# A chunked state-space scan with its state update turned round, its exponents made in pairs, and its loop written out

## The chip, the cores and the metric

The kernel runs on one core of a Trainium2 chip. The time is device time from launch to end. The kernel before was timed three times: 3505.67, 3506.23 and 3528.6 us, median 3506.23 us.

## What is computed

Two layers on 2 x 2048 tokens of width 256: a state-space mixer, a mixture of experts, an attention without softmax, and a feed-forward with dequantized weights, each followed by a residual and a norm. The change touches the mixer, cut here to what matters (64 heads, 8 channels a head, 64 states):

```python
dt = softplus(dt_raw + dt_bias)
a = exp(-exp(A_log) * dt)
Bh = rope(rms(Braw) + B_bias, phi)          # phi = cumsum(dt) * rope_freqs, per head
Ch = rope(rms(Craw) + C_bias, phi)
u = xh * dt
def step(h, (a_t, u_t, b_t, c_t)):
    h = a_t * h + u_t outer b_t             # h: batch, head, 8 channels, 64 states
    y = einsum('bhpn,bhn->bhp', h, c_t)
```

## The kernel before

`project_and_decay` projects the tokens in 16 chunks of 128 tokens (both batches together) and writes B, C, phi, u, wu (u weighted by the decay to the end of the chunk), the running log decay in three bf16 pieces and their negatives, the decay since the chunk's start (et) and that of the whole chunk (dec) to scratch.

`state_space_scan` runs 64 steps t: 16 chunks c times 4 blocks k of 16 heads. A step has 4 quarters q of four heads (8 groups g of two heads, two groups a quarter). Chunks 0 and 15 are written out, chunks 1 to 14 are a hardware loop of four steps a pass. Each engine has its own list, written by hand and tied by semaphores:

- ScalarE: `in_turns`, `whole_turns` (three activations a quarter), `magnitude`, `sines` make sine and cosine of the angles three and two steps ahead; the sine needs one table and the exponential another, so two table loads a step. `decays` turns a bank of exponents into decays D (L837); `turned` copies a bank of turned B into BT (L843).
- SyncE: `expand` spreads sine and cosine over partitions with 16 DMAs a step; `load_g` fetches the exponent pieces, `load_phi`, `load_u`, `load_wu`, `load_last` the rest. One queue in order.
- VectorE: `products` (four operations a group, L914 and L920), then `decayed`: M = scores times D, a bank each (L928), `outputs`, `new_state` (four small operations: state times dec, plus the new part).
- GpSimd: adds the products to C and B turned by the angle (CR L627, BR L633), spreads u into uexp, subtracts whole turns (L618).
- TensorE, by line: `exponents` (one 512-column bf16 mask matmul at L662 over all rows and two 256-column ones of 15 rows at L665, for one bank; eight banks a step), `turned` (four 128x128 fp32 transposes, L676), `scores` (eight fp32 matmuls in two halves of the rows, L688), `outputs` (`of_chunk` L703 and `of_state` L696, 32 columns of the array each), `new_state` (four fp32 matmuls with the turned B as the stationary side and 16 moving columns, L733). An fp32 matmul that isn't a transpose is two passes, two records in the trace.

Exponents and turned B share two PSUM banks, `x_ps[0]` and `x_ps[1]`, in turn: an item may be written when the item two before it has been read by ScalarE (`at_least(e, S["x_ok"], t, per, i - 1)`). The score banks `sc_ps` are single.

## Time and profile before

| | |
|---|---|
| median of three runs | 3506.23 us |
| the profiled execution, time / span | 3547.34 / 3545.6 us |
| busy share of the span: TensorE, VectorE, ScalarE, GpSimd | 80%, 57%, 43%, 40% |
| mean granted clock of TensorE | 0.776 |
| `project_and_decay` | to about 222 us |
| the scan | 225 to about 2206 us |
| the rest | 2206 to 3545 us |

The profile is one execution; the granted clock is 1.0 at 2.4 GHz and 0.5 at 1.2 GHz. Records on TensorE overlap, since matmuls are pipelined: a group of matmuls is best read from the start of one row to the start of the next. A few matmul records are missing (half of those of L662), which shows as idle time with "issue" behind it.

### The profile page before, as it was taken

To read this page: it belongs to the slowest core of one execution; us is meant where nothing else is said; L and a number is where in the kernel's file an instruction comes from. 1 tells how busy PE (TensorE), PEld (TensorE's weight loads), DVE (VectorE), ACT (ScalarE), POOL (GpSimd) and SP (SyncE) were. 2 spreads that over 40 slices of the span, in tenths; PEclk is the share of its full clock that TensorE was granted. 3 is DMA by queue.
4 is the path that set the end of the run, shared out by engine and by line. 5 is a ranking of instruction groups with operands and counts; after the bars stand their busy time and mean duration, and the time that the engine had idled before them with its cause. 6 is when DMAs were issued, how large, how long until landed. Compare 5 with 4: busy or idle time off the path is not lost. (4 is left out here: it accounts for less than half of the span.)

```text
span 3545.6 us, 70494 instructions
## 1 busy us (share of the span) xinstructions
PE 2838.9 (80%) x20132; PEld 2130.3 (60%) x20386; DVE 2018.2 (57%) x5459; ACT 1542.2 (43%) x3010; POOL 1435.4 (40%) x2256
## 2 busy tenths in 40 slices
PE   7848888888888888888888888888683885775888
PEld 4526666666666666666666666677562443553887
DVE  4546666656666665666666665333462222774777
ACT  4455555555565555656665553111450111221222
POOL 2236554545554454555555453000240111441544
PEclk9876676766676676767776667899786998887999
DMA  5654444444444444444444443322343222333111
GB/s 152 181 159 118 114 113 115 116 103 110 108 113 98 116 116 105 116 112 114 111 118 112 99 99 82 96 91 92 117 139 125 68 70 85 105 112 110 36 44 39
DMA packets 320535, 374.69 MB, mean 106 GB/s; under 512 B 71314, under 2 KB 260980, under 8 KB 319796
## 3 DMA queue, kind: packets, MB, share of 16 engines
q1 hardware_dynamic: 310404, 344.02, 37.1%
q0 software_dynamic: 9872, 27.28, 2.3%
q8 instruction: 155, 2.54, 0.3%
q14 instruction: 104, 0.85, 0.1%
HBM read 150.33 MB, written 86.58 MB: 67 GB/s over the span
## 5 line engine op out<-in xcount | busy, mean ns | idle before, releaser
L627 POOL TENSOR_TENSOR p_CR<-p_pc 128x256 f32<-128x256 f32 x512 | 372.8, 728 | 713.7 <-DVE p_pc L914 653.9
L928 DVE TENSOR_TENSOR p_M<-p_ps_sc,p_D 128x512 f32<-128x512 f32 x512 | 329.6, 686 | 562.6 <-PE p_ps_sc L688 561.6
L688 PE MATMUL p_ps_sc<-p_CR,p_BR 64*128 64x128 f32 x4096 | 445.6, 381 | 4.7 <-POOL p_BR L633 4.3
L843 ACT ACTIVATE p_BT<-p_ps_x 128x512 f32<-128x512 f32 x256 | 151.5, 592 | 619.6 <-PE p_ps_x L676 619.6
L688 PEld LDWEIGHTS p_ps_sc<-p_CR,p_BR 64*128 64x128 f32 x4096 | 382.2, 276 | 60.6 <-issue 40.5
L703 PE MATMUL p_ps_y<-p_M,p_uexp 128*32 128x128 f32 x4096 | 374.0, 342 | 31.4 <-issue 31.4
L837 ACT ACTIVATE p_D<-p_ps_x 128x512 f32<-128x512 f32 x512 | 303.7, 594 | 195.6 <-PE p_ps_x L665 127.1
L633 POOL TENSOR_TENSOR p_BR<-p_pb 128x256 f32<-128x256 f32 x512 | 371.8, 726 | 37.4 <-DVE p_pb L920 22.7
L733 PEld LDWEIGHTS p_ps_ns<-p_wu,p_BT 128*128 128x128 f32 x2048 | 335.7, 249 | 73.5 <-issue 52.5
L733 PE MATMUL p_ps_ns<-p_wu,p_BT 128*128 128x16 f32 x2048 | 361.5, 312 | 0.0
L676 PE MATMUL p_ps_x<-p_ident,p_BR 128*128 128x128 f32 x1024 | 224.4, 358 | 138.6 <-ACT p_D L837 138.6
L665 PE MATMUL p_ps_x<-p_GR,p_GL 15*128 15x256 bf16 x1024 | 244.2, 327 | 109.4 <-issue 63.3
L703 PEld LDWEIGHTS p_ps_y<-p_M,p_uexp 128*32 128x32 f32 x4096 | 265.4, 136 | 73.4 <-issue 37.0
L914 DVE SCALAR_TENSOR_TENSOR p_pc<-p_ps_c,p_beta,p_cs 128x256 f32<-128x256 f32 x512 | 243.8, 476 | 54.6 <-DMA p_sn<-p_tr_s 25.5
L618 POOL TENSOR_TENSOR p_tr_s<-p_xt,p_mg 128x256 f32<-128x256 f32 x256 | 186.9, 730 | 203.5 <-ACT p_mg L818 203.5
L696 PE MATMUL p_ps_y<-p_CR,p_ST 128*32 128x128 f32 x2048 | 264.9, 347 | 0.0
L676 PEld LDWEIGHTS p_ps_x<-p_ident,p_BR 128*128 128x128 f32 x1024 | 144.2, 178 | 195.9 <-ACT p_D L837 139.4
L920 DVE SCALAR_TENSOR_TENSOR p_pb<-p_ps_b,p_beta,p_cs 128x256 f32<-128x256 f32 x512 | 243.3, 475 | 0.0
L914 DVE SCALAR_TENSOR_TENSOR p_pc<-p_ps_c,p_beta,p_sn 128x256 f32<-128x256 f32 x512 | 243.3, 475 | 0.0
L920 DVE SCALAR_TENSOR_TENSOR p_pb<-p_ps_b,p_beta,p_sn 128x256 f32<-128x256 f32 x512 | 243.3, 475 | 0.0
L665 PEld LDWEIGHTS p_ps_x<-p_GR,p_GL 15*128 15x128 bf16 x1024 | 59.1, 97 | 179.6 <-issue 179.6
L1677 PE MATMUL p_ps_up<-p_w,p_xT 128*128 x288 | 130.3, 576 | 43.7 <-issue 43.0
(279 smaller groups left out, 5324.8 us busy)
## 6 DMA issues: line engine op xcount, KB each, us to landing
p_cs<-p_tr_c SPq DMA_DIRECT2D x512, 128.0 KB, 2.4
p_sn<-p_tr_s SPq DMA_DIRECT2D x512, 128.0 KB, 2.4
p_phib<-scratch_phi SPq DMA_DIRECT2D x256, 128.0 KB, 2.9
p_x<-scratch_rt SPq DMA_DIRECT2D x72, 128.0 KB, 2.0
scratch_ro<-p_o POOLq DMA_DIRECT2D x72, 128.0 KB, 2.0
p_xT<-in_xT SPq DMA_DIRECT2D x64, 128.0 KB, 3.0
scratch_u<-p_u SPq DMA_DIRECT2D x16, 512.0 KB, 3.8
scratch_wu<-p_wu SPq DMA_DIRECT2D x16, 512.0 KB, 5.0
```

Source lines behind the costliest of these rows:

```text
L627: e.tensor_tensor(CR[:, p, g, :], pc[:, g % 2, 0, :], pc[:, g % 2, 1, :], ALU.add).then_inc(S["rotC"], 1)
L633: e.tensor_tensor(BR[:, g, :], pb[:, g % 2, 0, :], pb[:, g % 2, 1, :], ALU.add).then_inc(S["rotB"], 1)
L665: m = e.matmul(bank[:, :].rearrange("p (g b l) -> p g b l", g=2, b=BATCH)[:, :, b, :], GL[:, p, cols], GR[:, p, half:4:2, cols], start=Fal ...
L676: m = e.transpose(x_ps[i % 2][:, (g * 2 + b) * P:(g * 2 + b + 1) * P], BR[:, 2 * q + g, b * L:(b + 1) * L], ident[:, :])
L688: m = e.matmul(sc_ps[half][:, (g * 2 + b) * L:(g * 2 + b + 1) * L], BR[half * 64:half * 64 + 64, 2 * q + g, b * L:(b + 1) * L], CR[half * ...
L696: m = e.matmul(yx_ps[32 * q:32 * q + 32, b * L:(b + 1) * L], ST[:, k, q, b, g, :], CR[:, k % 2, 2 * q + g, b * L:(b + 1) * L], start=(g == ...
L703: m = e.matmul(yi_ps[32 * q:32 * q + 32, b * L:(b + 1) * L], uexp[:, p, b, 4 * q + h, :], M[:, m_slot(p, 2 * q + h % 2), (h // 2 * 2 + b) ...
L733: m = e.matmul(ns_ps[:, ((q * 2 + b) * 2 + g) * 16:((q * 2 + b) * 2 + g) * 16 + 16], BT[:, q, g * 2 + b, :], wu[:, p, b, (2 * q + g) * 16: ...
L837: e.activation(D[:, n, :], x_ps[i % 2][:, :], ACT.Exp).then_inc(S["x_ok"], 1)
L914: e.scalar_tensor_tensor(out=pc[:, g % 2, n - 2, :], in0=c_ps[:, (n - 2) * CT:(n - 1) * CT], scalar=beta[:, k, n, g:g + 1], in1=tr[:, p, g ...
L920: e.scalar_tensor_tensor(out=pb[:, g % 2, n, :], in0=b_ps[:, n * CT:(n + 1) * CT], scalar=beta[:, k, n, g:g + 1], in1=tr[:, p, g % 2, g // ...
L928: e.tensor_tensor(M[:, m_slot(p, n), :], sc_ps[n % 2][:, :], D[:, n, :], ALU.mult).then_inc(S["m_ok"], 1)
```

## The change

- `project_and_decay` no longer makes the decay of the whole chunk: one 128-column fp32 matmul, half of the exponent product, one exponential, two copies and one DMA a chunk go. `sufA_ok` is then signalled once a chunk.
- The state is held twice. SR is the state turned: partitions are (head, channel), the free side the 128 state rows; VectorE updates it from PSUM in two operations a step, with the last column of et as its decay. `state(t - 2)` transposes it on TensorE through one of the two shared banks, and ScalarE copies the needed blocks to ST, which `of_state` reads as before.
- `new_state` is one group a step: wu is the stationary side in four column tiles of 32, the turned B moves with 256 columns. Eight matmuls instead of sixteen.
- `exponents` makes two banks at once: the mask as four matmuls of 256 columns in two halves of the rows, the exponents as four of 256 columns with 16 rows each at rows 0 and 32. It waits until both banks have been read. Its operands come with eight DMAs a step instead of six; that of dec is gone.
- No loop: all 64 steps are written out on all engines, with constants for waits and addresses. The last four steps make no new state.
- The order within a step is new on TensorE, ScalarE and GpSimd.

```diff
-                at_least(e, S["sufA_ok"], t, 2, 0)
+                at_least(e, S["sufA_ok"], t, 1, 0)
                 for b in range(BATCH):
                     e.matmul(ph_ps[0:NH, b * L:(b + 1) * L], dtp[:, b, :], triu[:, :], start=True, stop=True)
                     e.matmul(ph_ps[0:NH, CT + b * L:CT + (b + 1) * L], dt[:, b, :], triu[:, :], start=True, stop=True)
-                e.matmul(cum_ps[:, 0:2 * NH], tril[:, :], dt[:, :, :].rearrange("p b h -> p (b h)"), start=True, stop=True)
-                e.matmul(cum_ps[:, 2 * NH:4 * NH], ones[:, :], dt[:, :, :].rearrange("p b h -> p (b h)"),
-                         start=True, stop=True).then_inc(S["cum_mm"], 1)
+                e.matmul(cum_ps[:, 0:2 * NH], tril[:, :], dt[:, :, :].rearrange("p b h -> p (b h)"), start=True, stop=True
+                         ).then_inc(S["cum_mm"], 1)
...
-                at_least(e, S["dec_ok"], t, 1, 0)
-                for n in range(2):
-                    e.tensor_tensor(expo[:, n, :, :], cum_ps[:, n * 2 * NH:(n + 1) * 2 * NH].rearrange("p (b h) -> p b h", b=BATCH),
-                                    repeat(nA_bc[:, :], BATCH), ALU.mult).then_inc(S["sufA_ok"], 1)
+                e.tensor_tensor(expo[:, :, :], cum_ps[:, 0:2 * NH].rearrange("p (b h) -> p b h", b=BATCH),
+                                repeat(nA_bc[:, :], BATCH), ALU.mult).then_inc(S["sufA_ok"], 1)
...
-                for h in range(2):
-                    e.tensor_copy(decx[h * 64:(h + 1) * 64, p, :, :, :],
-                                  dec[h * 64:(h + 1) * 64, :, :].rearrange("p b (q e h) -> p q b e h", e=2, h=2)[:, :, :, :, h]
-                                  ).then_inc(S["decx_ok"], 1)
...
-        GR = sb("GR", [15, 2, 4, NQ * CT], BF16)
-        GL = sb("GL", [15, 2, NQ * CT], BF16)
+        GR = sb("GR", [48, 2, 2, NQ * CT], BF16)
+        GL = sb("GL", [48, 2, NQ * CT], BF16)
...
-        ST = sb("ST", [P, NB, NQ, BATCH, 2, 32])
+        SR = sb("SR", [P, NB, BATCH, 2, P])
+        ST = sb("ST", [P, NB, 2, BATCH, P])
...
+        order = [("D", 0, n) for n in range(4)]
+        for t in range(T):
+            order += [("B", t - 1, 2)] * (1 <= t <= LAST) + [("D", t, 4), ("D", t, 5)]
+            order += [("B", t - 1, 3)] * (1 <= t <= LAST) + [("D", t, 6), ("D", t, 7)]
+            order += [("S", t - 2, 0)] * (2 <= t < LAST + 2) + [("B", t, 0)] * (t < LAST)
+            order += [("D", t + 1, 0), ("D", t + 1, 1)] * (t + 1 < T) + [("B", t, 1)] * (t < LAST)
+            order += [("D", t + 1, 2), ("D", t + 1, 3)] * (t + 1 < T)
+        place = {item: i for i, item in enumerate(order)}
...
+                for half in range(2):
+                    r = 32 * half
+                    e.dma_start(GR[r:r + 3, p, :, :], W["pieces"][c].rearrange("a (h k q) t -> a h k (q t)", h=4, k=NB)[:, half:4:2, k, :]
+                                ).then_inc(g_in[p], 16)
+                    for a in range(3):
+                        e.dma_start(GL[r + 3 + 4 * a:r + 7 + 4 * a, p, :],
+                                    W["negs"][c, a].rearrange("(h k q) t -> h k (q t)", h=4, k=NB)[:, k, :]).then_inc(g_in[p], 16)
...
-                    stage_u(t, p, g // 2, g % 2)
-                    if 1 <= g <= NQ and ahead:
-                        turns(t + 2, p, g - 1)
+                    if g % 2:
+                        if g < NG - 1 and t + 2 < T:
+                            turns(t + 2, p, g // 2 + 1)
+                        if g == NG - 1 and t + 3 < T:
+                            turns(t + 3, 1 - p, 0)
+                        for b in range(BATCH):
+                            stage_u(t, p, g // 2, b)
...
+            def exponents(t, p, q):
+                n = 2 * q
+                i = place["D", t, n]
                 if n == 0:
+                    at_least(e, g_in[p], t - p, 8 * 8, 16 * 8)
+                at_least(e, S["x_ok"], i, 1, 0)
+                bank = [x_ps[(i + half) % 2] for half in range(2)]
+                for turn in range(2):
+                    for half in range(2):
+                        r = slice(64 * half, 64 * half + 64)
+                        e.matmul(bank[half][:, :].rearrange("p (n l) -> p n l", l=L)[:, :, 64 * turn:64 * turn + 64], eye[r, turn, :],
+                                 repeat(low[r, :], 4), start=(turn == 0), stop=False)
+                for b in range(BATCH):
+                    at = slice(q * CT + b * L, q * CT + b * L + L)
+                    for half in range(2):
+                        r = 32 * half
+                        m = e.matmul(bank[half][:, :].rearrange("p (g b l) -> p g b l", g=2, b=BATCH)[:, :, b, :], GL[r:r + 16, p, at],
+                                     GR[r:r + 16, p, :, at], start=False, stop=(b == 1))
+                        if b:
+                            m.then_inc(S["x_mm"], 1)
...
+
+            def state(t):
+
+                i = place["S", t, 0]
+                at_least(e, S["st_ok"], t, 2, 2)
+                at_least(e, S["x_ok"], i, 1, -1)
+                for g in range(2):
+                    for b in range(BATCH):
+                        m = e.transpose(x_ps[i % 2][:, (g * 2 + b) * P:(g * 2 + b + 1) * P], SR[:, t % NB, b, g, :], ident[:, :])
...
+            def new_state(t, p):
+                at_least(e, S["x_ok"], place["B", t, NQ - 1], 1, 1)
+                at_least(e, wu_got[p], t - p, 8, 16)
+                at_least(e, S["st_ok"], t, 2, 0)
+                for b in range(BATCH):
+                    for q in range(NQ):
+                        m = e.matmul(ns_ps[32 * q:32 * q + 32, b * CT:(b + 1) * CT], wu[:, p, b, 32 * q:32 * q + 32],
+                                     BT[:, q, b:4:2, :], start=True, stop=True)
+                        if b:
+                            m.then_inc(S["ns_mm"], 1)
...
-                later = not (isinstance(t, int) and t == 0)
-                more = not (isinstance(t, int) and t == T - 1)
-                if later:
-                    outputs(l, lk, 0, 1)
+                kept, more = t <= LAST, t + 1 < T
+                scores(t, p, 0)
+                if t and kept:
                     turned(l, 2)
-                scores(t, p, 0)
-                if later:
-                    exponents(t, p, 4)
-                    exponents(t, p, 5)
-                    new_state(l, lp, 1)
+                exponents(t, p, 2)
+                if t:
                     outputs(l, lk, 1, 0)
+                scores(t, p, 1)
+                if t and kept:
                     turned(l, 3)
-                scores(t, p, 1)
-                exponents(t, p, 6)
-                exponents(t, p, 7)
-                if later:
-                    new_state(l, lp, 2)
+                exponents(t, p, 3)
+                if t:
                     outputs(l, lk, 1, 1)
-                    new_state(l, lp, 3)
                 scores(t, p, 2)
-                turned(t, 0)
+                if t and kept:
+                    new_state(l, lp)
+                if 2 <= t < LAST + 2:
+                    state(t - 2)
+                if t < LAST:
+                    turned(t, 0)
                 if more:
                     exponents(t + 1, 1 - p, 0)
-                    exponents(t + 1, 1 - p, 1)
                 outputs(t, k, 0, 0)
                 scores(t, p, 3)
-                turned(t, 1)
+                if t < LAST:
+                    turned(t, 1)
+                outputs(t, k, 0, 1)
                 if more:
-                    exponents(t + 1, 1 - p, 2)
-                    exponents(t + 1, 1 - p, 3)
-                new_state(t, p, 0)
-
+                    exponents(t + 1, 1 - p, 1)
...
+            for t in range(T):
+                step(t, t % NB, t // NB)
...
+                if t and t <= LAST:
+                    turned(t - 1, 2)
+                for q in range(2):
+                    if q and t and t <= LAST:
+                        turned(t - 1, 3)
+                    decays(t, 4 + 2 * q)
...
+            def state(t):
+
+                i = place["S", t, 0]
+                at_least(e, S["x_mm"], i, 1, 1)
+                at_least(e, S["yx_mm"], t, U, U)
+                for h in range(2):
+                    r = slice(h * 64, h * 64 + 64)
+                    def own(ap):
+                        return bass.AP(tensor=ap.tensor, offset=ap.offset, ap=[list(ap.ap[0]), [2 * P + 16, 2], [32, BATCH * NQ], [1, HD]])
+                    e.activation(own(ST[r, t % NB, 0, 0, h * HD:h * HD + HD]), own(x_ps[i % 2][r, h * HD:h * HD + HD]), ACT.Copy
+                                 ).then_inc(S["x_ok" if h else "kept"], 1)
...
-                for h in range(2):
-                    r = slice(h * 64, h * 64 + 64)
-                    e.tensor_tensor(state_blocks(k, r, h), state_blocks(k, r, h),
-                                    spread(dec[r, p, :].rearrange("p (n e) -> p n e", e=2), HD), ALU.mult).then_inc(S["st_dec"], 1)
+                at_least(e, et_in[p], t - p, 8, 16)
                 at_least(e, S["ns_mm"], t, NQ, NQ)
-                at_least(e, S["st_dec"], t, 2, 2)
-                for h in range(2):
-                    r = slice(h * 64, h * 64 + 64)
-                    e.tensor_tensor(state_blocks(k, r, h), state_blocks(k, r, h),
-                                    ns_ps[r, 0:NQ * BATCH * 32].rearrange("p (n e d) -> p n e d", e=2, d=16)[:, :, :, h * HD:(h + 1) * HD],
-                                    ALU.add).then_inc(S["st_ok"], 1)
+                if t >= NB:
+                    e.wait_ge(S["x_mm"], place["S", t - NB, 0] + 1)
+                for b in range(BATCH):
+                    s = SR[:, k, b, :, :].rearrange("p g n -> p (g n)")
+                    e.scalar_tensor_tensor(out=s, in0=s, scalar=et[:, p, b * L + L - 1:b * L + L], in1=ns_ps[:, b * CT:(b + 1) * CT],
+                                           op0=ALU.mult, op1=ALU.add).then_inc(S["st_ok"], 1)
...
```

TensorE, one middle step before, from the third scores group (names: ps_sc scores, ps_x the shared banks, ps_ns the new state, ps_y outputs):

```order
L688 MATMUL p_ps_sc<-p_CR,p_BR 128x128 x8
L676 MATMUL p_ps_x<-p_ident,p_BR 128x128 x4
L662 MATMUL p_ps_x<-p_mask,p_identb 128x512
L665 MATMUL p_ps_x<-p_GR,p_GL 128x2x128 x2
L662 MATMUL p_ps_x<-p_mask,p_identb 128x512
L665 MATMUL p_ps_x<-p_GR,p_GL 128x2x128 x2
L703 MATMUL p_ps_y<-p_M,p_uexp 32x128 x4
L696 MATMUL p_ps_y<-p_CR,p_ST 32x128 x2
L703 MATMUL p_ps_y<-p_M,p_uexp 32x128 x4
L696 MATMUL p_ps_y<-p_CR,p_ST 32x128 x2
L688 MATMUL p_ps_sc<-p_CR,p_BR 128x128 x8
```

The same place now:

```order
L692 MATMUL p_ps_sc<-p_CR,p_BR 128x128 x8
L738 MATMUL p_ps_ns<-p_BT,p_wu 32x256 x8
L681 MATMUL p_ps_x<-p_ident,p_SR 128x128 x4
L670 MATMUL p_ps_x<-p_ident,p_BR 128x128 x4
L652 MATMUL p_ps_x<-p_low,p_eye 128x4x64 x4
L658 MATMUL p_ps_x<-p_GR,p_GL 128x2x128 x4
L707 MATMUL p_ps_y<-p_M,p_uexp 32x128 x4
L700 MATMUL p_ps_y<-p_CR,p_ST 32x128 x2
L707 MATMUL p_ps_y<-p_M,p_uexp 32x128 x4
L700 MATMUL p_ps_y<-p_CR,p_ST 32x128 x2
L692 MATMUL p_ps_sc<-p_CR,p_BR 128x128 x8
```

The four groups of new state that stood apart are one behind the third scores, the state's transposes follow, and the pair of banks is filled by one group of eight.

ScalarE around the sines before (D decays, BT turned B, xt and mg the turns of the angles, tr_s and tr_c sine and cosine):

```order
L843 ACTIVATE p_BT<-p_ps_x 128x512
L822 ACTIVATE p_tr_c<-p_tr_s 128x512
L828 ACT_TABLE_LOAD
L828 ACTIVATE p_tr_c<-p_tr_c,p_quart 128x512 x2
L831 ACTIVATE p_tr_s<-p_tr_s 128x512 x2
L837 ACT_TABLE_LOAD
L837 ACTIVATE p_D<-p_ps_x 128x512
L811 ACTIVATE p_xt<-p_phib,p_fsc 128x256
L837 ACTIVATE p_D<-p_ps_x 128x512
```

And now:

```order
L829 ACTIVATE p_D<-p_ps_x 128x512
L803 ACTIVATE p_xt<-p_phib,p_fsc 128x256
L829 ACTIVATE p_D<-p_ps_x 128x512
L808 ACTIVATE p_mg<-p_phib,p_fsc 128x256
L810 ACTIVATE p_mg<-p_mg 128x256
L814 ACTIVATE p_tr_c<-p_tr_s 128x512
L820 ACT_TABLE_LOAD
L820 ACTIVATE p_tr_c<-p_tr_c,p_quart 128x512 x2
L823 ACTIVATE p_tr_s<-p_tr_s 128x512 x2
L835 ACTIVATE p_BT<-p_ps_x 128x512
L829 ACT_TABLE_LOAD
L829 ACTIVATE p_D<-p_ps_x 128x512
```

The copy of turned B that stood ahead of the sines stands behind them, ahead of the second table load.

## Rows read from the trace of the kernel before

**Rows 1.** Busy time by stretch: length, PE, PEld, DVE, ACT, POOL, clock, DMA, GB/s.

```profile
428.20:2106.90 1678.70, 1442.38 (x12542) 1068.65 (x12761) 1078.97 (x2530) 978.55 (x1816) 866.65 (x1540) 0.70 0.46 111
2206.00:3545.00 1339.00, 989.10 (x4865) 776.22 (x4865) 636.90 (x2174) 304.15 (x705) 359.53 (x402) 0.87 0.28 89
```

**Rows 2.** Instruction groups, 428 to 2107 us: busy us, mean ns | idle before, releaser.

```profile
L928 DVE TENSOR_TENSOR p_M<-p_ps_sc,p_D 128x512 f32<-128x512 f32 x440 | 283.3, 686 | 495.6 <-PE p_ps_sc L688 494.8
L676 PE MATMUL p_ps_x<-p_ident,p_BR 128*128 128x128 f32 x880 | 194.3, 360 | 121.0 <-ACT p_D L837 121.0
```

**Rows 3.** TensorE in order of time at clock 1.0: start, length, instruction, count.

```profile
1007.05 0.39 PE L665 MATMUL p_ps_x<-p_GR,p_GL 15*128 15x256 bf16 x2 [0.26 <-issue]
1007.69 0.39 PE L665 MATMUL p_ps_x<-p_GR,p_GL 15*128 15x256 bf16 x2
1008.00 1.06 PE L733 MATMUL p_ps_ns<-p_wu,p_BT 128*128 128x16 f32 x8
1009.00 0.30 PE L703 MATMUL p_ps_y<-p_M,p_uexp 128*32 128x128 f32 x2
...
1010.00 1.06 PE L733 MATMUL p_ps_ns<-p_wu,p_BT 128*128 128x16 f32 x8
...
1016.40 1.16 PE L688 MATMUL p_ps_sc<-p_CR,p_BR 64*128 64x128 f32 x16
1017.49 0.66 PE L676 MATMUL p_ps_x<-p_ident,p_BR 128*128 128x128 f32 x4
```

**Rows 4.** The same at clock 0.5.

```profile
1032.90 0.60 PE L665 MATMUL p_ps_x<-p_GR,p_GL 15*128 15x256 bf16 x2 [0.48 <-issue]
1033.97 0.60 PE L665 MATMUL p_ps_x<-p_GR,p_GL 15*128 15x256 bf16 x2
1034.50 1.89 PE L733 MATMUL p_ps_ns<-p_wu,p_BT 128*128 128x16 f32 x8
1036.32 0.43 PE L703 MATMUL p_ps_y<-p_M,p_uexp 128*32 128x128 f32 x2
...
1038.17 1.89 PE L733 MATMUL p_ps_ns<-p_wu,p_BT 128*128 128x16 f32 x8
1039.99 2.08 PE L688 MATMUL p_ps_sc<-p_CR,p_BR 64*128 64x128 f32 x16
1042.01 1.11 PE L676 MATMUL p_ps_x<-p_ident,p_BR 128*128 128x128 f32 x4
```

**Rows 5.** Busy time by stretch, between changes of the granted clock.

```profile
1024.30:1031.10 6.80, 4.56 (x57) 3.35 (x58) 4.42 (x10) 6.74 (x11) 2.36 (x5) 1.00 0.36 80
1031.10:1048.20 17.10, 16.27 (x120) 11.97 (x122) 10.84 (x26) 6.54 (x14) 7.83 (x14) 0.50 0.56 135
```

**Rows 6.** ScalarE in order of time, around the sines.

```profile
1024.48 1.28 ACT L828 ACT_TABLE_LOAD   x1
...
1029.46 0.60 ACT L837 ACTIVATE p_D<-p_ps_x 128x512 f32<-128x512 f32 x1
...
1031.69 0.58 ACT L843 ACTIVATE p_BT<-p_ps_x 128x512 f32<-128x512 f32 x1
```

**Rows 7.** VectorE in order of time: outputs of steps 0 and 4, written-out steps.

```profile
304.71 0.42 DVE L954 TENSOR_TENSOR p_y<-p_ps_y,p_yx 128x256 f32<-128x256 f32 x1
...
428.20 0.42 DVE L954 TENSOR_TENSOR p_y<-p_ps_y,p_yx 128x256 f32<-128x256 f32 x1
```

**Rows 8.** VectorE in order of time, one quarter of a step.

```profile
1014.88 0.48 DVE L914 SCALAR_TENSOR_TENSOR p_pc<-p_ps_c,p_beta,p_cs 128x256 f32<-128x256 f32 x1
...
1018.03 1.28 DVE L928 TENSOR_TENSOR p_M<-p_ps_sc,p_D 128x512 f32<-128x512 f32 x2
1019.22 0.47 DVE L914 SCALAR_TENSOR_TENSOR p_pc<-p_ps_c,p_beta,p_cs 128x256 f32<-128x256 f32 x1
```

**Rows 9.** SyncE's queue in order of time.

```profile
1002.13 5.25 SPq L521 DMA_DIRECT2D p_cs<-p_tr_c  x8
```

**Rows 10.** Instruction groups of the first phase, 20 to 220 us.

```profile
L399 DVE COPY p_decx<-p_dec 64x64 f32<-64x64 f32 x32 | 21.1, 661 | 0.5
```

More of the change, by code:

```diff
@@ L584, in _ @@
                 step(k, k, 0)
-            with e.Fori(1, NC - 1) as c:
+            for c in range(1, NC - 1):
                 for k in range(NB):
@@ L771, in step @@
-                new_state(t, p, 0)
-            for n in range(EARLY):
-                exponents(0, 0, n)
-            for k in range(NB):
-                step(k, k, 0)
-            with e.Fori(1, NC - 1) as c:
-                for k in range(NB):
-                    step(c * NB + k, k, c)
-            for k in range(NB):
-                step(T - NB + k, k, NC - 1)
-            t, k, p = T - 1, NB - 1, 1
-            outputs(t, k, 0, 1)
-            turned(t, 2)
-            turned(t, 3)
-            new_state(t, p, 1)
@@ L879, in _ @@
                 sines(s, s)
-            for n in range(EARLY):
+            for n in range(4):
                 decays(0, n)
@@ L884, in _ @@
                 step(k, k, 0)
-            with e.Fori(1, NC - 1) as c:
+            for c in range(1, NC - 1):
                 for k in range(NB):
@@ L976, in _ @@
                 step(k, k, 0)
-            with e.Fori(1, NC - 1) as c:
+            for c in range(1, NC - 1):
                 for k in range(NB):
```

271 lines of the change are left out of this document (118 added, 153 removed).

## The prediction

> **What bounds the kernel now.** I read the table of stretches first. The 55 steps between 428 and 2107 us take 1678.7 us, 30.5 each; per step TensorE is busy 26.2 us, VectorE 19.6, ScalarE 17.8, GpSimd 15.8 [rows 1]. So TensorE carries most of the scan, and at a mean granted clock of 0.70: two fifths of the time at 2.4 GHz, three fifths at 1.2. The list of groups says the same from the other side: VectorE's largest wait is for scores (495 us), TensorE's own largest visible one is 121 us for ScalarE to free a shared bank [rows 2]. Then I read TensorE in order of time, once at either clock, start of group to start of group.
>
> At 2.4 GHz [rows 3]: one bank of exponents 0.64, a group of new state 1.00, of outputs 1.00, of scores 1.09, of turned B 0.59 (0.66 less the 0.07 that overlaps the next). At 1.2 GHz [rows 4]: 1.07, 1.82, 1.85, 2.02, 1.04. A step has eight banks and four of each other group: 5.1 + 4.0 + 4.0 + 4.4 + 2.4 = 19.8 us fast; 8.6 + 7.3 + 7.4 + 8.1 + 4.2 = 35.5 us slow. Half of each is 27.6, near the 26.2 us busy. The other 4.3 us are waits.
>
> **TensorE's work after.** Scores, turned B and outputs stay: 10.7 fast, 19.6 slow.
> *New state.* Four groups go (4.0, 7.3). One comes: eight matmuls of two passes, 256 columns each, in four column tiles. No row has just this form. Nearest are the outputs, also four column tiles of 32: there the longest tile has eight passes of 128 columns, here four of 256, the same 1024 columns. I take 1.0 fast, 1.9 slow. If the tiles ran one after the other it would be four times that, 4.0 and 7.4: no gain.
> *Exponents.* A bank streams 512 + 2 x 256 = 1024 columns in 0.64 us; at 2.4 GHz the columns alone are 0.43. A pair of banks now streams eight times 256 columns, two at a time in different rows: again 1024 if the pairs run side by side. Scores are made of such halves: sixteen passes take 1.09 us where four whole-array passes take 0.59 [rows 3], so halves do overlap. Bounds for a pair: 0.64 (1.07) and 1.28 (2.14). I take 0.75 (1.3), near the lower end because of the scores, more than it for the extra weight loads. Four pairs: 3.0 and 5.2 instead of 5.1 and 8.6.
> TensorEngine Tiling of the Trainium skill, Key Properties, says that changing the tiling mode drains the engine. The 0.21 us above the columns in a bank would be two such changes; by that rule new modes beside old ones could cost some 0.1 us each, but the changes inside the exponents halve from sixteen to eight, so by it the pair is no dearer than I take.
> *State.* Four transposes, as turned B: 0.6, 1.0.
> Sum: 10.7 + 1.0 + 3.0 + 0.6 = 15.3 fast; 19.6 + 1.9 + 5.2 + 1.0 = 27.7 slow. TensorE loses 4.5 to 7.8 us a step.
>
> **What becomes late next.** (a) A pair waits for both banks. Three of the four pairs stand right behind a group of turned B, so TensorE waits until ScalarE has copied that: 0.58 us of copy [rows 6] and two hand-overs, about 0.8. That is 2.4 us a step, where before the second bank alone waited.
> (b) The sines. Behind the first pair ScalarE does D, xt, D, mg, mg (2.2 us, as from 1029.5 to 1031.7), an absolute value (0.6), table and sines (4.98 less the second load of 1.28: 3.7), the copy (0.6) [rows 6]: 7.1 us until the second pair may start. TensorE has outputs, scores, turned B, outputs to do: 3.7 us fast, 6.7 slow. So it idles 3 to 4 us fast, under 1 slow.
> (c) VectorE. A quarter of products takes 3.15 us, two banks of M 1.19 [rows 8]; four quarters, outputs (1.0) and the state make 19.4. Two state operations of 128x256, one source in PSUM, replace four of half the partitions: bounds nothing and twice 0.48, so at most 0.4 moves either way.
>
> Chain at 2.4 GHz from the end of the third scores: new state, state, turned B 2.2, copy 0.8, pair 0.75: 3.8. ScalarE 7.1: 11. Pair and scores: 13. Now VectorE: M 1.2, products 3.15, M 1.2, products 3.15, outputs 1.0: **22.7**, when the next third M comes. At 1.2 GHz TensorE has no rest: 27.7 + 2.4 + 0.8 = **31**.
>
> **The clock.** From 1024.3 to 1031.1 TensorE was busy for 4.56 of 6.8 us at 1.0, then the clock fell, and from 1031.1 to 1048.2 it was busy for 16.27 of 17.1 us at 0.5 [rows 5]. The stages behind the scan are at 0.87, busy for 989 of 1339 us [rows 1]. So these rows don't tell what other work in the scan will be granted; (b) opens an idle stretch each step at 1.0, as the one before the fall. I take the middle between the scan's 0.70 and the later 0.87: 0.78, 56% of the time fast. Step: 1 / (0.56/22.7 + 0.44/31) = 25.7 us. With 0.70: 27.1; with 0.9: 24.0.
>
> **The rest.** *No loop:* the four written-out steps from 304.71 to 428.20 took 30.9 us each, the looped ones 30.5 [rows 7, 1]. So writing out is worth nothing by itself. *SyncE:* two DMAs more, one less; eight of the sixteen DMAs that spread sine and cosine take 5.25 us to issue [rows 9], the 16 of them 10.5, and the other 16 to 18 of a step no more each: at most some 21 in one queue, below 25.7, without much to spare. Its wait for new state moves back by one scores group. *GpSimd:* same work, 15.8 us. *First phase:* the copies are 21.1 us in all [rows 10] and stand on VectorE between u and the next chunk's v, but TensorE's sum of squares ends nearly as late; between 0 and 22 us, I take 6. *Last four steps:* no turned B, new state, state (4 us less each for three) and the shorter step: 25.
> Sum: 60 steps x (30.5 - 25.7) = 288, + 25 + 6 = 319 us. The profiled execution took 3547.34 us; 3547 - 319 = 3228. It stands 41 us above the median of the runs, so against that: **3190 us**.
>
> **Rivals.**
> 1. *Forecast*, steps of 24 to 28.9 us, 3090 to 3390: chance 0.62.
> 2. *The clock stays up* through the idle stretch; then VectorE's chain of 22.7 rules: 60 x 7.8 + 50 = 518 less, 2990. For it: 0.87 behind the scan [rows 1]. Against: the idle stretch each step. 0.15.
> 3. *The clock falls.* Every step has an idle stretch after which the clock drops, and 31 us at 1.2 GHz is nearly reached: steps of 29 to 31, 3390 to 3510, priced 3450. For it: [rows 5]. Against: at 1.2 GHz the idle stretch shrinks to under 1 us, and before, the clock rose again in each step. 0.15. TensorE: Matmul & The Clock Gate (HAM oscillation) says that idle gaps between bursts put the clock back; by that rule it would be this rival, 3450, and this trace agrees at 1031.1.
> 4. *Slower: tiles do not run side by side.* New state 4.0 (7.4) and pairs 1.28 (2.14) make 20.4 fast and 36.7 slow, against 19.8 and 35.5 now: 0.9 us more work a step, and (a) adds 2.4, with all else kept a step of 33: 60 x 2.8 - 30 = +140, 3640. It decides once the gained overlap is worth less than the 2.4 us of new waits. Against it: outputs and scores overlap in just these tilings [rows 3]. 0.08.
>
> About 1% (35 us) is what a measurement here can tell from no change. Faster by more (under 3471): rivals 1, 2 and half of 3: 0.85. Same: 0.08. Slower: 0.07. The range reaches from 3000 to 3430: all of the forecast's own 3090 to 3390, the upper half of rival 2 and the lower half of rival 3.
>
> **What would show it.** Steps of 25 to 26 us between outputs. New state as one group of 1.0 (1.9) us; four to twice that would be rival 4. A pair of banks in 0.75 (1.3) us. TensorE idle before each pair: three times 0.8 for ScalarE's copy, once several us behind the sines. A clock of 0.78 in the scan: above 0.9 is rival 2, below 0.6 rival 3. VectorE's wait for scores down from 9 us a step to 6. The forecast is wrong if a DMA ends VectorE's waits, which would be SyncE's queue, or if VectorE's busy time grows by more than 0.4 us a step.

## The result, and the profile after

| | before | after |
|---|---|---|
| median, four runs each | 3517.41 us | 3166.49 us |
| lowest to highest | 3505.67 to 3550.91 | 3158.88 to 3191.54 |
| ratio, 95% interval | | 0.8998, 0.8924 to 0.9072 |
| profiled execution, time / span | 3547.34 / 3545.6 us | 3191.54 / 3189.9 us |
| first to last output of the scan | 304.7 to 2205.1: 1900.4 us | 321.8 to 1845.5: 1523.7 us |

A tenth of the time is gone: 3190 was forecast. Two further executions of the changed kernel took 3186.52 and 3149.3 us, so its six reach from 3149 to 3192 us, and the profiled one, 3191.54, is the slowest of them, 25 us above the median, so its steps are some 0.4 us longer than those of the median run (25 over 64 steps, an estimate). A run more than 1.5% above the fastest of its kernel counts as slow here, which holds for three of the four of a_halfwait below and for two of the four of a_single_both and of a_filler_busy. By the profiles the span lost 355.7 us: 376.7 between the first and the last output of the scan; ahead of it 17.1 came on top, behind it 3.9. Inside the scan the last four steps gave 30.6 (98.1 us before, 67.5 after, from output to output), the other 59 gave 346.1, 5.87 each (30.55 before, 24.68 after).

The stretches of after (length, PE, PEld, DVE, ACT, POOL, clock, DMA, GB/s), which answer to [rows 1]:

```profile
11.00:222.00 211.00, 180.54 (x603) 118.51 (x604) 92.37 (x270) 89.11 (x164) 52.59 (x43) 0.80 0.53 154
430.00:1778.00 1348.00, 1017.26 (x12408) 696.47 (x12409) 1043.26 (x2398) 992.84 (x1908) 875.92 (x1524) 0.79 0.56 137
1850.00:3189.00 1339.00, 991.49 (x4865) 778.77 (x4865) 635.52 (x2171) 302.98 (x705) 359.83 (x400) 0.87 0.28 89
```

In the scan TensorE is busy for 75% of the time, VectorE now for 77% and ScalarE for 74%: no engine stands out any more. The clock is 0.79, from 0.70. The outputs come in a pattern of four, 23.7, 23.8, 25.8 and 25.7 us, mean 24.75, which repeats through the scan:

```profile
887.11 0.42 DVE L971 TENSOR_TENSOR p_y<-p_ps_y,p_yx 128x256 f32<-128x256 f32 x1
912.81 0.42 DVE L971 TENSOR_TENSOR p_y<-p_ps_y,p_yx 128x256 f32<-128x256 f32 x1
936.52 0.42 DVE L971 TENSOR_TENSOR p_y<-p_ps_y,p_yx 128x256 f32<-128x256 f32 x1
960.32 0.42 DVE L971 TENSOR_TENSOR p_y<-p_ps_y,p_yx 128x256 f32<-128x256 f32 x1
986.11 0.43 DVE L971 TENSOR_TENSOR p_y<-p_ps_y,p_yx 128x256 f32<-128x256 f32 x1
```

TensorE in order of time, against [rows 3] and [rows 4]. A pair of banks at 2.4 GHz, with the new state and the state behind it; then a pair at 1.2 GHz:

```profile
989.69 0.39 PE L652 MATMUL p_ps_x<-p_low,p_eye 64*128 64x256 bf16 x4 [0.93 <-ACT p_BT L835]
990.02 0.39 PE L658 MATMUL p_ps_x<-p_GR,p_GL 16*128 16x256 bf16 x4
990.34 0.30 PE L707 MATMUL p_ps_y<-p_M,p_uexp 128*32 128x128 f32 x2
...
997.51 0.61 PE L652 MATMUL p_ps_x<-p_low,p_eye 64*128 64x256 bf16 x4 [3.42 <-ACT p_BT L835]
998.05 0.61 PE L658 MATMUL p_ps_x<-p_GR,p_GL 16*128 16x256 bf16 x4
998.59 0.58 PE L692 MATMUL p_ps_sc<-p_CR,p_BR 64*128 64x128 f32 x2
...
1010.98 1.07 PE L738 MATMUL p_ps_ns<-p_BT,p_wu 128*32 128x256 f32 x16
1011.98 0.66 PE L681 MATMUL p_ps_x<-p_ident,p_SR 128*128 128x128 f32 x4
```

Start to start: a pair takes 0.65 us (989.69 to 990.34) and 1.08 (997.51 to 998.59), all new state of a step 1.00 where four groups of that length stood. The brackets are the waits for ScalarE's copy of turned B. The long one, 3.42 us, is there because the copy stands behind the sines. ScalarE in order of time:

```profile
992.67 0.61 ACT L814 ACTIVATE p_tr_c<-p_tr_s 128x512 f32<-128x512 f32 x1
993.30 1.28 ACT L820 ACT_TABLE_LOAD   x1
994.60 1.33 ACT L820 ACTIVATE p_tr_c<-p_tr_c,p_quart 128x512 f32<-128x512 f32 x2
995.84 1.13 ACT L823 ACTIVATE p_tr_s<-p_tr_s 128x512 f32<-128x512 f32 x2
996.88 0.57 ACT L835 ACTIVATE p_BT<-p_ps_x 128x512 f32<-128x512 f32 x1
```

The groups, 430 to 1778 us (busy us, mean ns | idle before, releaser), against [rows 2]:

```profile
L950 DVE TENSOR_TENSOR p_M<-p_ps_sc,p_D 128x512 f32<-128x512 f32 x436 | 280.1, 684 | 283.1 <-PE p_ps_sc L692 283.0
L652 PE MATMUL p_ps_x<-p_low,p_eye 64*128 64x256 bf16 x872 | 106.3, 330 | 326.6 <-ACT p_BT L835 326.6
```

Eight M a step, so the 436 are 54.5 steps: VectorE waits 5.2 us a step for scores instead of 9, TensorE 6.0 for the copies. All of that is near the forecast, which says nothing yet on why the time fell. The experiments take that up. Where a kernel is called "the changed kernel with ...", all else is as in it.

### The profile page after: what moved, and what is told of

Read it like the earlier page. It is cut to its first block and busy times, and to the rows that moved or that the text cites. A ratio compares the mean times of both kernels' runs of the same rounds, so it can differ in the third digit from the quotient of the medians.

```text
span 3189.9 us, 63590 instructions
## 1 busy us (share of the span) xinstructions
PE 2361.8 (74%) x19953; PEld 1713.3 (54%) x19954; DVE 1962.2 (62%) x5279; ACT 1555.5 (49%) x3098; POOL 1455.4 (46%) x2255
## 5 line engine op out<-in xcount | busy, mean ns | idle before, releaser
L652 PE MATMUL p_ps_x<-p_low,p_eye 64*128 64x256 bf16 x1024 | 124.8, 330 | 408.2 <-ACT p_BT L835 359.6
L692 PE MATMUL p_ps_sc<-p_CR,p_BR 64*128 64x128 f32 x4096 | 377.7, 336 | 13.4 <-POOL p_BR L615 7.8
L615 POOL TENSOR_TENSOR p_BR<-p_pb 128x256 f32<-128x256 f32 x512 | 373.5, 730 | 25.8
L692 PEld LDWEIGHTS p_ps_sc<-p_CR,p_BR 64*128 64x128 f32 x4096 | 322.4, 236 | 86.3 <-issue 49.3
L707 PE MATMUL p_ps_y<-p_M,p_uexp 128*32 128x128 f32 x4096 | 341.7, 321 | 5.1 <-POOL p_uexp L592 3.9
L652 PEld LDWEIGHTS p_ps_x<-p_low,p_eye 64*128 64x128 bf16 x1024 | 34.1, 100 | 479.9 <-ACT p_BT L835 360.0
L707 PEld LDWEIGHTS p_ps_y<-p_M,p_uexp 128*32 128x32 f32 x4096 | 244.7, 128 | 82.4 <-issue 65.3
L670 PE MATMUL p_ps_x<-p_ident,p_BR 128*128 128x128 f32 x960 | 187.8, 328 | 4.6 <-ACT p_D L829 3.1
L1660 POOL DMA_DIRECT2D scratch_ro<-p_o x72 | 39.2, 544 | 276.3 <-DVE p_o L1764 272.5
L1758 DVE TENSOR_TENSOR p_h<-p_sa,p_ps_up 128x224 f32<-128x224 f32 x72 | 27.9, 388 | 190.7 <-ACT p_sa L1739 190.7
L2298 ACT ACTIVATE p_sg<-p_ps_g,p_gs 128x256 f32<-128x256 f32 x128 | 53.8, 471 | 185.7 <-PE p_ps_g L2236 185.7
```

Source lines behind the costliest of these rows:

```text
L615: e.tensor_tensor(BR[:, g, :], pb[:, g % 2, 0, :], pb[:, g % 2, 1, :], ALU.add).then_inc(S["rotB"], 1)
L652: e.matmul(bank[half][:, :].rearrange("p (n l) -> p n l", l=L)[:, :, 64 * turn:64 * turn + 64], eye[r, turn, :], repeat(low[r, :], 4), sta ...
L670: m = e.transpose(x_ps[i % 2][:, (g * 2 + b) * P:(g * 2 + b + 1) * P], BR[:, 2 * q + g, b * L:(b + 1) * L], ident[:, :])
L692: m = e.matmul(sc_ps[half][:, (g * 2 + b) * L:(g * 2 + b + 1) * L], BR[half * 64:half * 64 + 64, 2 * q + g, b * L:(b + 1) * L], CR[half * ...
L707: m = e.matmul(yi_ps[32 * q:32 * q + 32, b * L:(b + 1) * L], uexp[:, p, b, 4 * q + h, :], M[:, m_slot(p, 2 * q + h % 2), (h // 2 * 2 + b) ...
```

## The experiments

Twelve kernels, with the changed kernel in the first row. Each ratio is to the kernel before, run beside it on the same chip. The kernels of the table did not all run on one chip, so two of them are best compared by their ratios, and the clock is that of one profiled execution each.

| kernel | median, us (lowest to highest) | ratio, 95% interval | clock, 430 to 1630 us |
|---|---|---|---|
| the changed kernel | 3166.5 (3158.9 to 3191.5) | 0.8998, 0.8924 to 0.9072 | 0.79 |
| b_unrolled | 3570.8 (3565.2 to 3572.6) | 1.0125, 1.0080 to 1.0171 | 0.67 |
| a_oldboth | 3198.3 (3197.9 to 3212.2) | 0.9109, 0.9067 to 0.9151 | 0.80 |
| a_oldstate | 3288.6 (3281.8 to 3299.1) | 0.9323, 0.9268 to 0.9379 | 0.77 |
| a_single | 3131.3 (3128.2 to 3141.3) | 0.8889, 0.8836 to 0.8942 | 0.84 |
| a_single_both | 3335.5 (3278.6 to 3365.3) | 0.9345, 0.9230 to 0.9460 | 0.76 |
| a_halfwait | 3186.2 (3136.3 to 3189.7) | none given | 0.79 |
| a_oldphase0 | 3158.6 (3149.5 to 3161.9) | 0.8959, 0.8918 to 0.8999 | 0.82 |
| a_copy_first | 3135.0 (3132.1 to 3147.3) | 0.8883, 0.8815 to 0.8951 | 0.86 |
| a_filler | 3129.9 (3129.2 to 3130.4) | 0.8860, 0.8795 to 0.8924 | 0.86 |
| a_filler_busy | 3250.9 (3207.9 to 3275.0) | 0.9268, 0.9213 to 0.9324 | 0.88 |
| a_copy_filler | 3128.6 (3121.6 to 3138.2) | 0.8907, 0.8865 to 0.8948 | 0.94 |
| a_copy_single | 3212.3 (3209.6 to 3220.6) | 0.9133, 0.9097 to 0.9170 | 0.82 |

### The loop alone: b_unrolled

```diff
-            with e.Fori(1, NC - 1) as c:
+            for c in range(1, NC - 1):
```

> The kernel before with its five hardware loops of the scan written out, and nothing else. My theory (the gain is less TensorE work and better overlap, the loop costs nothing): steps of 30 to 31 us, the time within 1% of before, 3480 to 3555. Rival (the loop costs each engine a stop at every fourth step): steps of 29 or less, 60 us or more gone, under 3455.

Slower by 1.25%, which neither theory had: the rival expected a gain, mine a time within 1%. The steps themselves are nearly as long as before: almost all 30.7 us, one like the other, where the looped ones vary between 26 and 34 with a mean of 30.5. In the profiles 13.0 us of the 24.2 come ahead of the first output (317.7 for 304.7) and 10.8 in the scan. The first phase, whose code is the same, differs from 55 us on; the kernel before, then this one:

```profile
55.00:100.00 45.00, 36.79 (x159) 23.74 (x158) 27.76 (x81) 24.08 (x47) 12.94 (x11) 0.99 0.72 205
```

```profile
55.00:100.00 45.00, 40.37 (x128) 26.12 (x127) 21.98 (x64) 18.53 (x36) 11.23 (x10) 0.73 0.55 156
```

At 0.73 instead of 0.99 TensorE gets through 128 matmuls instead of 159. All written-out kernels here have their first output later than 304.7, at 309.1 to 329.1. But the clock of this stretch is no mark of the written-out loop: with the same first phase it is 0.97 in a_oldboth, 0.85 in a_oldstate and 0.82 in a_oldphase0, each in one execution. What makes the clock fall earlier in some of them was not found.

### The order without the lighter work: a_oldboth, a_oldstate

a_oldstate puts the old state back (and with it the old first phase); a_oldboth fills banks singly as well, so that TensorE again has the work of the kernel before.

```diff
-                for b in range(BATCH):
-                    for q in range(NQ):
-                        m = e.matmul(ns_ps[32 * q:32 * q + 32, b * CT:(b + 1) * CT], wu[:, p, b, 32 * q:32 * q + 32],
-                                     BT[:, q, b:4:2, :], start=True, stop=True)
+                for q in range(NQ):
+                    for g in range(2):
+                        for b in range(BATCH):
+                            m = e.matmul(ns_ps[:, ((q * 2 + b) * 2 + g) * 16:((q * 2 + b) * 2 + g) * 16 + 16], BT[:, q, g * 2 + b, :],
+                                         wu[:, p, b, (2 * q + g) * 16:(2 * q + g) * 16 + 16], start=True, stop=True)
...
-                if 2 <= t < LAST + 2:
-                    state(t - 2)
```

> The changed kernel with the old handling of the state: sixteen narrow fp32 matmuls of new state, here in one place, VectorE's four small operations with the decay of the whole chunk, no transposes of the state, and the first phase of before. Pairs, order and written-out steps stay. My theory (TensorE's work decides): four groups of 1.0 (1.82) instead of one of 1.01 and a transpose group of 0.6 (1.0): 2.4 us fast and 4.4 us slow more a step, a third of it hidden in the idle stretch behind the sines: steps of 26.5 to 28.5, the time 3270 to 3400. Rival (pairs and order made the whole gain): 3150 to 3210.

> The new order and the written-out steps alone: single banks as in a_single, the old handling of the state and the old first phase as in a_oldstate. TensorE then has the work of the kernel before, 19.8 us a step at 2.4 GHz and 35.5 at 1.2. Theory A (the forecast's sum: less work in TensorE is the gain): nothing is left of it, 3480 to 3570, steps of 29.5 to 31. Theory B (the order is most of the gain: single banks cost nothing in it, the old state 120 to 140 us): 3230 to 3300, steps of 25 to 26.5, at a clock of 0.80 or more in the scan.

a_oldstate came where the theory had it, which looked like support for it. a_oldboth overturns it: with the whole old work on TensorE the time is 3198 us, below even theory B's range. The same stretch, 430 to 1630 us, and groups of it, of the kernel before:

```profile
430.00:1630.00 1200.00, 1030.09 (x8962) 762.83 (x9116) 771.49 (x1810) 697.50 (x1296) 617.32 (x1097) 0.70 0.46 111
...
L928 DVE TENSOR_TENSOR p_M<-p_ps_sc,p_D 128x512 f32<-128x512 f32 x316 | 203.4, 686 | 356.0 <-PE p_ps_sc L688 355.5
L676 PE MATMUL p_ps_x<-p_ident,p_BR 128*128 128x128 f32 x632 | 139.5, 359 | 85.2 <-ACT p_D L837 85.2
```

and of a_oldboth:

```profile
430.00:1630.00 1200.00, 1157.71 (x11499) 821.71 (x11492) 934.04 (x2206) 844.75 (x1582) 770.76 (x1343) 0.80 0.56 136
...
L938 DVE TENSOR_TENSOR p_M<-p_ps_sc,p_D 128x512 f32<-128x512 f32 x384 | 246.8, 685 | 152.6 <-PE p_ps_sc L698 151.4
L743 PE MATMUL p_ps_ns<-p_wu,p_BT 128*128 128x16 f32 x1536 | 210.0, 285 | 0.0
L686 PE MATMUL p_ps_x<-p_ident,p_BR 128*128 128x128 f32 x768 | 158.8, 342 | 4.1 <-ACT p_D L831 3.3 <-POOL p_BR L633 0.4
```

316 and 384 M in the same time: 39.5 steps and 48, or 30.4 and 25.0 us each. TensorE is busy for 86% and 96% of the time; its wait of 85 us for ScalarE to read an exponent bank is 3.3; VectorE waits 3.2 us a step for scores instead of 9.0. Two things stand side by side here, and the rows allow an estimate of their shares. With 19.8 us of work at 2.4 GHz and 35.5 at 1.2, and four tenths of the time fast, as clock 0.70 says, a step is 1 / (0.4/19.8 + 0.6/35.5) = 27.0 us of work; with six tenths, clock 0.80, it is 24.1. So some 2.9 us of the 5.4 are the clock and the rest, 2.5, is idle time of TensorE that went.

This kernel keeps more of the change than the order: the steps written out (which alone cost), new state's groups in one place, the mask in halves. It does without the two parts that make TensorE's work less. Which of the moves within the order brings how much was not tried one by one.

### The pairs: a_single, a_single_both, a_halfwait

```diff
-                at_least(e, S["x_ok"], i, 1, 0)
-                bank = [x_ps[(i + half) % 2] for half in range(2)]
-                for turn in range(2):
-                    for half in range(2):
+                for half in range(2):
+                    at_least(e, S["x_ok"], i + half, 1, -1)
+                    bank = x_ps[(i + half) % 2]
+                    for turn in range(2):
```

and so on for the exponents: a_single fills one bank, then the other. a_single_both does the same behind one wait for both banks, `at_least(e, S["x_ok"], i, 1, 0)`. a_halfwait moves that wait into the masks' loop over banks and leaves the exponent matmuls in pairs. Its masks are then filled bank by bank and no longer run side by side: its TensorE is busy for 992 of the 1200 us, that of the changed kernel for 906.

> The changed kernel, its order and halves of rows kept, but the two banks of a pair filled one after the other, each when it is free. My theory (paired row tiles run side by side): the pair's 0.65 us becomes 1.28 and 1.08 becomes 2.1, so four pairs cost TensorE 2.5 to 4 us more a step, part of it given back because the first bank no longer waits for the second (three waits of 0.8): steps of 26 to 28 against 24.75, the time 3240 to 3370. Rival (the gain is all order and new state, the pairs are worth nothing, since the wait for both banks eats it): 3140 to 3190, as the changed kernel.

> The kernel with single banks (a_single, 3131 us, steps of 23.3, TensorE busy 20.4 us a step at clock 0.84), but each pair again waits for both banks before its first bank is filled. Theory A (the changed kernel's pairs lose by the wait for both banks, three times 0.8 us a step): the gain of a_single is gone: steps of 24.5 or more, 3190 or more, since the longer fill of 1.28 us comes on top. Theory B (they lose by the clock: less work in TensorE lets it fall, and more work keeps it up): the clock stays at 0.83 or above, steps of 23.3 to 24.2, 3130 to 3180.

> The changed kernel with pairs, but the mask of the first bank goes out when that bank is free, ahead of the wait for the second; the exponent matmuls stay paired. Theory A (the wait for both banks): some 0.3 us of four waits a step leave the path, steps of 23.7 to 24.4 against 24.75, 3130 to 3170, at an unchanged clock. Theory B (the clock): no change beyond what the clock does, 3150 to 3195 at 0.79.

Both theories on a_single were wrong: it is faster than the changed kernel. The difference is small, about 1% by the ratios, whose intervals just overlap, but the slowest of its four runs (3141.3 us) lies 8 us below the fastest of that kernel's six (3149.3). The price of two banks is as expected, 0.63 us each; TensorE of a_single in order of time:

```profile
983.52 0.38 PE L652 MATMUL p_ps_x<-p_low,p_eye 64*128 64x256 bf16 x2 [0.31 <-ACT p_ST L887]
983.83 0.39 PE L657 MATMUL p_ps_x<-p_GR,p_GL 16*128 16x256 bf16 x2
984.15 0.39 PE L652 MATMUL p_ps_x<-p_low,p_eye 64*128 64x256 bf16 x2
984.47 0.39 PE L657 MATMUL p_ps_x<-p_GR,p_GL 16*128 16x256 bf16 x2
```

So TensorE has 2.5 us more work a step, and the steps are 23.7 instead of 24.8 (by the estimate above some 0.4 us of that is the changed kernel's profile, which isn't its median run). With the old state the pairs cost even more: a_oldstate is 90 us behind a_oldboth. a_single_both shows what they cost by: the same fills, but behind the wait for both banks, and its fastest run is 137 us above a_single's slowest. The wait is what hurts. VectorE's wait for scores goes from 197.5 to 342.8 us of the 1200, 3.9 to 8.0 us a step, so the late pair is passed on to it. Theory B, steps of 24.2 at most at a clock that stays up, is refuted by the time; the 0.76 of the table is from its slowest run, 3365 us. Filling side by side makes good a part of what that wait costs, not all of it. a_halfwait decides nothing: three of its runs are at 3184 to 3190 us, one at 3136, on either side of the changed kernel's median, and what its earlier first mask could gain stands against masks that are no longer side by side.

### The idle stretch and the clock: a_copy_first, a_filler, a_filler_busy, a_copy_filler

a_copy_first, ScalarE's list:

```diff
+                if t < LAST:
+                    turned(t, 1)
                 if t + 2 < T:
                     magnitude(t + 2, p, 1)
                     sines(t + 2, p)
-                if t < LAST:
-                    turned(t, 1)
```

a_filler, TensorE's list, with GB a tile of ones; in a_filler_busy the same stands behind `scores(t, p, 2)`, in a_copy_filler twelve of them behind `scores(t, p, 0)`:

```diff
                 outputs(t, k, 0, 1)
+                if 1 <= t < LAST:
+                    at_least(e, S["st_ok"], t, 2, 0)
+                    for n in range(8):
+                        e.matmul(ns_ps[:, :], eye[:, 0, :], GB[:, :], start=True, stop=True)
                 if more:
                     exponents(t + 1, 1 - p, 1)
```

> The changed kernel with ScalarE's copy of the second turned B back ahead of the magnitude and the sines, as in the kernel before. Theory (the wait of the second pair, 3.4 us a step, is for this copy, which stands behind 3.7 us of sines): TensorE can start the pair 3 us sooner, but ScalarE must wait for scores and turned B ahead of the sines, 1.9 us at 2.4 GHz and 3.9 at 1.2, and is then late for the next exponentials: between 1 us a step gained and 2 lost, 3100 to 3290, most likely 3200 with the clock above 0.82. Rival (the sines' place costs nothing, VectorE sets the step): 3155 to 3185.

> The changed kernel plus eight bf16 matmuls of 512 columns a step that nothing reads, some 1.7 us at 2.4 GHz and 3.4 at 1.2, put on TensorE where it waits 3.4 us for ScalarE behind the sines. Theory B (idle stretches cost the clock): the granted clock in the scan goes from 0.79 to 0.84 or more and the steps from 24.75 to 23 to 24: 3060 to 3140. Rival (TensorE has no time to give): the filler lengthens the steps that run at 1.2 GHz, 3190 to 3260.

Useless work in the idle stretch makes the kernel 37 us faster than the changed one, and its four runs lie within 1.2 us. The steps are 23.9 and the clock 0.86, as theory B had it; the clock still falls once in each step, though TensorE's longest wait is now 2.0 us. a_copy_first gains 32 us without extra work, in the time's own range but better than its likeliest value. Both are about 1%: all their runs lie below all six of the changed kernel, while the intervals of the ratios touch or overlap. In a_copy_first every step but the first few is 23.9, and the clock falls once in each. Two of its stretches between changes of the clock:

```profile
1005.03:1022.10 17.07, 12.35 (x190) 8.70 (x186) 15.82 (x37) 12.66 (x23) 11.21 (x19) 1.00 0.64 155
1022.10:1028.92 6.82, 4.79 (x42) 3.08 (x44) 3.21 (x9) 5.30 (x12) 4.71 (x10) 0.50 0.93 205
```

TensorE has its one long pause around the fall, from 1019.2 to 1023.1, and the group behind the pause runs at 1.2 GHz (1.09 us in place of 0.66); TensorE in order of time:

```profile
1018.00 1.16 PE L692 MATMUL p_ps_sc<-p_CR,p_BR 64*128 64x128 f32 x16 [0.15 <-DVE p_M L950]
1023.09 1.09 PE L670 MATMUL p_ps_x<-p_ident,p_BR 128*128 128x128 f32 x4 [3.93 <-ACT p_D L829]
```

> The control of a_filler: the same eight matmuls that nothing reads, but behind the third scores, where TensorE isn't idle, and the idle stretch behind the sines stays. Theory (it is the idle stretch that counts, not how busy TensorE is over the step): 1.8 us more work on the path and no fewer falls: the scan's clock stays below 0.82, steps of 25 to 26.5, 3190 to 3290. Rival (any work in the step keeps the clock up): 3130 to 3160 as a_filler.

> a_copy_first (steps of 23.9, the clock falls once a step, behind TensorE's one long idle stretch of 3.9 us after the first scores) with twelve bf16 matmuls of 512 columns, 2.8 us at 2.4 GHz, that nothing reads, in that stretch. Theory (the idle stretch is what lets the clock fall, and without falls VectorE's chain sets the step, forecast at 22.7): clock 0.93 or more, steps of 22 to 23, 3030 to 3090. Rival (the clock falls for another reason, as often): steps of 23.9 or longer, 3130 to 3200.

The control was half right. The time is in the theory's range, its two fastest runs (3208 and 3242 us) 41 and 76 us above the changed kernel's median (0.917 of the kernel before; the table's ratio is of its three slower ones); the clock is not: 0.88, higher than with the filler in the pause, although a wait of 3.43 us behind the sines is still there. So the pause alone does not set the clock. Matmuls in either place kept it up; only those in the pause cost nothing. a_copy_filler adds to the picture. The clock is at 0.94, and the time, 3128.6, is that of a_copy_first within 0.3% (the rival's time, at the theory's clock); the steps are mostly 23.7 to 23.9, as at 0.86. But most of these steps still hold a fall, of 3.4 us instead of a_copy_first's 6.8. Three steps in a row, from output to output, the first two without a fall; then VectorE in order of time in another step without one:

```profile
624.37:646.63 22.26, 17.59 (x247) 11.67 (x240) 19.04 (x45) 17.99 (x35) 16.02 (x29) 1.00 0.69 169
646.63:668.88 22.25, 17.58 (x247) 11.66 (x240) 19.04 (x44) 19.22 (x39) 16.07 (x29) 1.00 0.62 146
668.88:692.67 23.79, 19.05 (x247) 12.64 (x240) 18.95 (x44) 17.99 (x35) 16.01 (x29) 0.93 0.57 137
```

```profile
1062.66 0.48 DVE L949 SCALAR_TENSOR_TENSOR p_pb<-p_ps_b,p_beta,p_sn 128x256 f32<-128x256 f32 x1
1066.80 1.29 DVE L956 TENSOR_TENSOR p_M<-p_ps_sc,p_D 128x512 f32<-128x512 f32 x2 [3.66 <-PE p_ps_sc L694]
```

Eight of the 59 steps have no fall, and they take 22.2 to 22.7 us. So the theory's 22 to 23 is right for a step at full clock, and what failed is that the falls would be gone: the filler took them out of eight steps only. Why a fall of 3.4 us leaves the step as long as one of 6.8 no run shows. Within the steps at full clock VectorE still waits, here 3.66 us, for the scores that stand behind the sines, the copy and the pair: to get below 22 us their order would have to change as well.

### Both gains together: a_copy_single

Both edits shown above.

> Both moves that gained by themselves: ScalarE's copy ahead of the sines, and single banks in place of pairs. If they gain in the same way (a clock that falls less, 35 us each), the sum isn't theirs: 3100 to 3140, steps of 23.3 to 23.9. If they add: 3090 or less, steps under 23. If the fills of 1.28 us are in the way once the long wait is gone: 3150 or more.

The third case: 3212.3, steps of 24 to 27.5. The two moves don't add, they spoil each other. In the profile VectorE waits 261.9 of 1200 us for scores, 5.5 us a step, where a_single has 3.9; which of the waits ahead of those scores does it was not followed up.

### The first phase: a_oldphase0

The added lines of the diff of `project_and_decay` are taken out again, its removed ones are back; the scan is untouched and nothing reads the decay of the whole chunk.

> The changed kernel with the first phase of before: the decay of the whole chunk is computed, spread and stored again, and not used. The forecast gave 6 us for leaving it out (bounds 0 and 22), but the first output of the changed kernel came 17 us later than before, at a clock of 0.80 against 0.90. Theory A (the work left out was hidden, and the late output is the clock): the time is the changed kernel's, within 15 us either way, first output at 304 to 322. Theory B (leaving it out moves the first phase's rhythm into the slower clock): this kernel's first output is back at about 305 and the time 10 to 20 us less.

The time is 8 us below the changed kernel's, with intervals that overlap (0.8918 to 0.8999 and 0.8924 to 0.9072): no difference that is shown, as theory A had it. The first output was at 309.1, which fits both. That the first phase gains by doing less is not borne out. Its profile shows something else: the scan, the same instructions in the same order, took 1503.6 us instead of 1523.7. Of 59 steps 16 are above 25 us, in the changed kernel 27. So the pattern belongs to when the clock falls as much as to the code, and a difference of 20 us between two profiles, of which one is the changed kernel's slowest execution, is no evidence on an edit.

## Why the prediction came out, and where it was wrong

**The number held, its main step did not.** The forecast made 288 of its 319 us from steps 4.8 us shorter. By its own "With 0.70: 27.1" 3.4 of these are the shorter chains, for which TensorE was to lose 4.5 to 7.8 us of work a step, and 1.4 the higher clock. The new order got no term of its own. The runs put it otherwise, in ratios to the kernel before: the order, with the steps written out, 1 to 0.911; the new state (with the first phase) 0.911 to 0.889; the pairs 0.889 to 0.900. Nine tenths of the gain is there with the old work. Of the two parts that lighten TensorE the new state gives 67 us on top of single banks (122 on top of pairs, a_oldstate), and the pairs take 35 (90 with the old state). The failed step is in the reading of what bounds the kernel: "The other 4.3 us are waits" was all that was said of them. No chain was worked out for the old work in the new order, and so no term stood for waits that an order can take out. That step was 25.0 us where the forecast had 25.7 for all of the change. What the order removed was the waits, 121 us of which stood in [rows 2] by name, and with them went part of the time at 1.2 GHz: by the estimate above 2.5 and 2.9 us a step. That the total came within 1% is partly luck: the order's gain was left out, that of the lighter work was counted too high, and the two nearly cancel.

**Parts that were right.** New state as one group of 1.0: 1.00. A pair of banks: 0.65 and 1.08, the lower bound of 0.64 (1.07) where 0.75 (1.3) was taken; the tiles run fully side by side, and rival 4 is out. A pair still takes 0.22 us more than its columns, as a bank took 0.21. The Trainium skill (TensorEngine Tiling, Key Properties) says that a change of tiling mode drains the engine. Two changes in a pair at 0.1 us each would fit the 0.22, but no run here separates them from the start of a group. Waits ahead of the pairs, three times 0.8: 0.93, 0.69, 0.69; behind the sines 3 to 4: 3.42. Step 25.7: 24.75, of which the pairs' lower price explains 4 x 0.10 to 4 x 0.22 us. VectorE's wait for scores 6: 5.2, its busy time 19.2.

**The pair's wait was weighed on TensorE alone.** Part (a) had 2.4 us a step for it, against 2.1 to 3.4 us that the pairs save by the same text, and took both into one chain. By measured lengths the pairs save more, 2.5 us at 2.4 GHz (5.1 - 4 x 0.65), and still a_single, without the saving and with a wait for each bank by itself, is faster. The text priced what stands behind a late pair for the sines only; in a_single_both, with the wait for both banks, VectorE waits 8.0 us a step for scores, in a_single 3.9.

**The clock.** The mean of 0.78 was the middle between two rows, with no reason for the middle; that the profile shows 0.79 is luck, the more so as that execution is the slowest of six (mean clock of the whole 0.821, the others up to 0.841). Rival 3 went by idle gaps between bursts that put the clock back, the rule of the Trainium skill (TensorE: Matmul & The Clock Gate, HAM oscillation). It is borne out in part: in a_copy_first a fall comes in each pause of about 4 us, but in a_filler it comes once a step with no wait above 2.0 us, and in a_filler_busy the clock is 0.88 with the pause of 3.43 us left in. Its time, 3450, was wrong, since the clock rises again inside each step. Rival 2, the clock up and steps of 22.7 by VectorE's chain, did not come about. Its length of a step is borne out by a_copy_filler, whose copy stands ahead of the sines: 22.2 to 22.7 us in the steps at full clock, and 23.7 to 23.9 in most others.

**No loop, nothing.** True of the steady step (30.7 for 30.5), not of the kernel: 1.25% slower. **First phase, 6 us:** by the profile the first output is 17 us later; undoing this part moved the time by nothing that is shown. **Last four steps, 25:** 30.6. **SyncE's queue:** VectorE waited for DMAs 8.0 us in all between 430 and 1778 us, so it did not become the bound.

## What to carry to other kernels

When an engine is busy for most of a stretch at a clock that changes, its busy time is no measure of its work. Price the work at either clock, and ask of idle time and clock together what a new order of the same work could win back, before any work is removed. Before a part is credited with a gain, put its old work back into the new order; a forecast that lands can rest on the wrong part. And merging two fills into one is paid for by a wait for both buffers: it gains only where the time saved is more than what that wait costs the engines behind it. Here it was not.
